# Masked attention stages: VectorE caps the exponentials of every second key block's first pair by a table, in place of TensorE's mask products

## The chip, the cores and the metric

One core of a Trainium2 chip runs the whole program. The metric is device time in microseconds (us) of one execution; the time before is the median of three runs.

## The reference

Four decoder layers run one after the other on x of shape (4, 512, 256): L0 (two attentions with lengths, a small feed-forward), L1 (two masked attentions, then a mixture of experts), L2 (two masked attentions, then a feed-forward), L3 (a causal attention). The change touches the four masked attentions, those of L1 and L2. Cut to what matters:

```python
scores = jnp.einsum('bhqd,bhkd->bhqk', q, k) / jnp.sqrt(jnp.float32(DK))     # 16 heads, DK = 16
scores = jnp.where(mask[:, None, :, :] == 0, NEG, scores)                    # mask of shape (4, 512, 512)
attn = jax.nn.softmax(scores, axis=-1)
out = jnp.einsum('bhqk,bhkd->bhqd', attn, v)
```

## The kernel before

**Stages and units.** The seven attentions are the stages a0 to a6; a2 and a3 (L1) and a4 and a5 (L2) are masked. A stage takes the four batch elements one after the other. Each has four *units* (u = 0 to 3) of four heads, and a unit has eight *halves* (h = 0 to 7): half h belongs to key block kb = h // 2 (128 keys) and to the first or second pair of the unit's heads (h % 2). So the masked stages have 4 x 4 x 4 = 64 units and 512 halves.

**What a half does.** In unit j, TensorE computes for half h the transposed scores, keys on partitions (`key_scores`, L927: two products into one of two double banks of PSUM), then for unit j + 2 the scores with queries on partitions (`query_scores`, L966: two products into a ring of three banks), then for masked stages the mask products of unit j (`key_penalties`, L948: four products of 64 x 64 identity blocks with the transposed mask, added to the transposed scores). VectorE takes the row minimum of each ring bank with the mask added (L1225; scores are held negated), which unit j + 2 will need as its softmax shift, and so frees the bank. ScalarE takes the exponentials of the transposed scores (L1117) into `probT`, which has two slots, one for even and one for odd key blocks. In every even half TensorE multiplies a finished key block of `probT` by V (`outputs`, L987): h = 2, 4 and 6 take the blocks 0, 1 and 2, and the next unit's h = 0 takes block 3. This product waits for the exponentials of both pairs of its block.

**What sets the order.** All engines walk one list made by `schedule` from `timetable`: for each half "ST" (L927), "S" (L966), "exp" (L948 and L1117), then the side work of that half, then "PV" (L987). Side work goes through the same ring of three banks, in the order of the list: in unit 0 the outputs of the batch element before (transposes L1088 and L1092, the output projection L1097, VectorE's reciprocal L1293 and product L1304, and in a4 and a5 a layer norm); in unit 1 the projections q (h = 1) and k (h = 4) of the second half of the heads (L1043); in unit 2 the projection V (h = 1 and 4, L1050) and three of the four mask transposes "mT" (L1056, copied out by ScalarE at L1178); in unit 3 the fourth mT and the transposes of x (L1024) in h = 0, q (h = 4) and k (h = 6). Each unit also turns the minima of another unit (L1232, L1234, then L1011). The last batch element of a block of stages has no next one to prepare, and its units 2 and 3 have no "S" either.

**GpSimd and the DMA queue.** GpSimd turns each mask from integers to bfloat16 (L886, two halves of a batch element) and does parts of the norms. SyncE loads the weights of the coming feed-forward or expert stage into `raw` during a0, a2 and a4 (`load_feed`).

## Time and profile before

| | us |
|---|---|
| median of three runs (2736.17 to 2740.03) | 2736.99 |
| span of the profiled execution | 2740.1 |
| a2 and a3, from their first to their last half, about | 612 (664 to 1276) |
| a4 and a5, about | 606 (1770 to 2376) |
| TensorE busy, whole span | 2505.0 (91%) |
| VectorE busy, whole span | 1783.8 (65%) |
| ScalarE busy, whole span | 1397.9 (51%) |

The page gives the span of the profiled execution, from its first to its last instruction, and no other time for it; it lies 3 us above the median of the runs. "Busy" of TensorE counts a product from its issue to its modelled end, so that consecutive products overlap: the time from one start to the next is what a product costs.

### The profile page before, as it was taken

The page shows a single profiled execution, that of the slowest core. Times are in us where ns is not written, and L with a number is a line of the kernel's source. Part 1 is how long each engine was busy: PE and PEld are TensorE (multiplying, and loading weights), DVE is VectorE, ACT ScalarE, POOL GpSimd, SP SyncE. Part 2 cuts the span into 40 slices and gives each one's busy share as a digit, 9 for nine tenths or more (in the row PEclk, how much of TensorE's full clock was granted, in tenths as well). Part 3 has the DMA queues.
Part 4 walks back from the last instruction along what each step waited for, and adds up shares of the span by engine and source line. Part 5 has one row for each costly group of instructions (what it writes and reads, how often), then busy time and mean ns, then how long its engine had stood idle before and what let it go on. Part 6 is the DMA issues. An engine that isn't in the chain of part 4 may idle for free. (4 is left out here: it accounts for less than half of the span.)

```text
span 2740.1 us, 44289 instructions
## 1 busy us (share of the span) xinstructions
PE 2505.0 (91%) x16014; PEld 1383.7 (50%) x16014; DVE 1783.8 (65%) x4364; ACT 1397.9 (51%) x1921; POOL 739.6 (27%) x867
## 2 busy tenths in 40 slices
PE   6999988989999999997999998799999999797896
PEld 3444433334344444443889998334444444386553
DVE  3566777777777777773557775577777777455554
ACT  1544455545555555565348786155555555452332
POOL 2233334432421111200115664202222111224012
PEclk7999999989999999998899999699999999999999
DMA  6222212112223323220127875423322322001331
GB/s 177 51 50 71 57 45 72 46 45 61 52 82 85 90 68 95 68 64 17 47 70 216 221 220 130 126 60 87 101 67 68 94 68 64 1 9 28 96 84 41
DMA packets 102213, 218.56 MB, mean 80 GB/s; under 512 B 19116, under 2 KB 35372, under 8 KB 100716
## 3 DMA queue, kind: packets, MB, share of 16 engines
q1 hardware_dynamic: 93164, 203.66, 27.0%
q0 software_dynamic: 8832, 12.06, 2.5%
q8 instruction: 129, 2.11, 0.3%
q14 instruction: 88, 0.72, 0.1%
HBM read 100.34 MB, written 12.58 MB: 41 GB/s over the span
## 5 line engine op out<-in xcount | busy, mean ns | idle before, releaser
L1117 ACT ACTIVATE probT_a<-scores 128x1024 f32<-128x1024 f32 (+3 forms) x832 | 786.7, 951 | 733.1 <-PE scores L948 445.2
L1225 DVE CUSTOM_DVE_ANT_0 ring<-ring,maskb_a 128x512 f32<-128x512 f32 x1024 | 680.5, 720 | 176.7 <-PE ring L966 171.1
L966 PE MATMUL ring<-stacks_a 64*128 64x512 f32 (+7 forms) x1664 | 468.3, 411 | 58.8 <-DVE negm_a L1223 26.0
L987 PE MATMUL outputs<-probT_a,V_a 128*32 128x512 f32 (+6 forms) x3328 | 445.6, 579 | 18.5 <-ACT probT_a L1117 9.5
L1223 DVE TENSOR_REDUCE negm_a<-ring 128x1 f32<-128x512 f32 (+3 forms) x640 | 330.8, 564 | 148.9 <-PE ring L972 109.4
L927 PE MATMUL scores<-stacks_a 64*128 64x512 f32 (+7 forms) x1664 | 411.2, 474 | 2.3 <-DMA stacks_a<-narrow_a 2.3
L927 PEld LDWEIGHTS scores<-stacks_a 64*128 64x128 f32 (+1 forms) x1664 | 164.3, 185 | 432.1 <-issue 322.6
L966 PEld LDWEIGHTS ring<-stacks_a 64*128 64x128 f32 (+1 forms) x1664 | 236.2, 191 | 176.6 <-DVE negm_a L1225 72.0
L886 POOL TENSOR_SCALAR maskb_a<-ints_a 128x1024 bf16<-128x1024 int32 x31 | 112.8, 3639 | 409.1 <-DMA ints_a<-in_mask 336.2
L896 POOL TENSOR_TENSOR ve<-mv,epsilon 128x1 f32<-128x1 f32 x96 | 18.2, 190 | 722.5 <-DVE mv L1192 722.5
L948 PE MATMUL scores<-maskT_a,identb 64*64 64x512 bf16 x1024 | 210.2, 401 | 0.0
L948 PE MATMUL scores<-swapped_a,identb 64*64 64x512 bf16 x1024 | 206.7, 401 | 0.0
L1277 DVE SCALAR_TENSOR_TENSOR parts_a<-ring,wcol,parts_a 128x512 fp32r<-128x512 f32 x112 | 83.9, 751 | 186.2 <-ACT parts_a L1166 186.2
L1043 PE MATMUL ring<-xT_a,wt 128*128 128x512 f32 x320 | 169.4, 657 | 25.4 <-DVE xT_a L1265 12.3
L2017 DVE TENSOR_TENSOR hidden_moe<-whole_moe,hidden_moe 128x512 fp32r<-128x512 f32 x124 | 85.9, 692 | 103.2 <-ACT whole_moe L1826 103.2
L1166 ACT ACTIVATE parts_a<-ring,wcol 128x512 fp32r<-128x512 f32 x112 | 77.0, 688 | 148.5 <-PE ring L1043 148.5
L987 PEld LDWEIGHTS outputs<-probT_a,V_a 128*32 128x32 f32 (+1 forms) x3328 | 74.0, 111 | 154.1 <-ACT probT_a L1117 74.0
L1696 PE MATMUL scores<-rowsT_moe,weights_moe 128*128 128x256 f32 x1104 | 147.5, 283 | 0.0
L1225 DVE DVE_READ_ACCUMULATOR2_ANT negm_a<- 128x1 f32 x1024 | 145.6, 142 | 0.0
L1696 PEld LDWEIGHTS scores<-rowsT_moe,weights_moe 128*128 128x128 f32 x1104 | 139.1, 192 | 0.0
L948 PEld LDWEIGHTS scores<-maskT_a,identb 64*64 64x64 bf16 x1024 | 57.8, 103 | 159.1 <-issue 159.1
L1826 ACT ACTIVATE hidden_moe<-scores 128x512 fp32r<-128x512 f32 x124 | 74.1, 598 | 119.4 <-PE scores L1689 59.4
(240 smaller groups left out, 3757.4 us busy)
## 6 DMA issues: line engine op xcount, KB each, us to landing
stacks_a<-parts_a SPq DMA_DIRECT2D x672, 128.0 KB
raw<-in_moew SPq DMA_DIRECT2D x92, 512.0 KB, 4.1
ints_a<-in_mask SPq DMA_DIRECT2D x31, 512.0 KB, 3.5
swapped_a<-maskT_a SPq DMA_DIRECT2D x32, 256.0 KB, 3.7
wt<-in_w SPq DMA_DIRECT2D x7, 1024.0 KB, 4.9
kvT_a<-in_ctxT SPq DMA_DIRECT2D x12, 512.0 KB, 3.3
wrow<-in_row SPq DMA_DIRECT2D x7, 512.0 KB, 6.0
stacks_a<-narrow_a SPq DMA_DIRECT2D x224, 8.0 KB
```

The costliest lines, as they stand in the source:

```text
L886: pool.tensor_scalar(maskb[:, j % 2, 2 * n:2 * n + 2, :], mask_half(j, n)[:, :, :], 0.0, BIG, ALU.is_equal, ALU.mult)\
L927: last = pe.matmul(scores_bank(j, h)[:, e, q0:S], K[rows, g, kb * P:(kb + 1) * P], Q[rows, g, q0:S], start=True, stop=not (a.causal or a.m ...
L948: last = pe.matmul(out[64 * c:64 * c + 64, :], identb[at, at], (maskT if c == e else maskS)[at, m % 2, kb, :], start=False, stop=True)
L966: last = pe.matmul(bank("S", j, n, e)[:, 0:w], Q[rows, g, qt * P:(qt + 1) * P], K[rows, g, 0:w], start=True, stop=not a.causal)
L987: last = pe.matmul(OB[x * slot:(x + 1) * slot, q0:S], V[:, m % 2, kb, c:c + slot], probT[:, kb % 2, x, q0:S], start=(kb == 0), stop=(kb == ...
L1043: last = pe.matmul(out[:, :], wt[:, k, kb, c0:c0 + P], src[:, kb, :], start=(kb == 0), stop=(kb == KB - 1))
L1117: act.activation(probT[:, kb % 2, 2 * p:2 * p + 2, q0:S], scores_bank(j, n)[:, :, q0:S], ACT.Exp, bias=0.0, scale=-1.0).then_inc(c_exp.sem, 1)
L1223: least = dve.tensor_reduce(out, sc, AX.X, ALU.min)
L1225: least = dve.tensor_tensor_reduce(sc, sc, maskb[:, m % 2, qt, :], 1.0, BIG * 2, ALU.add, ALU.min, out)
L1277: dve.scalar_tensor_tensor(out=parts[:, n, low[kind], :], in0=bank(kind, j, n)[:, :], scalar=wcol[:, k, col:col + 1], in1=parts[:, n, high ...
L1696: last = pe.matmul(bank[:, h * SL:(h + 1) * SL], w1(i, a, kb, 2 * q + h), rowsT[:, i % 2, c, kb, :], start=(kb == 0 and (a, c) == PARTS[0] ...
L2017: dve.tensor_tensor(hidden[:, s % 4, 1, :], whole[:, s % 2, :], hidden[:, s % 4, 0, :].bitcast(F32), ALU.subtract).then_inc(m_low, 1)
```

## The change

In the halves h = 2 and h = 6 of every unit of a masked stage (the first pair of key blocks 1 and 3), TensorE's four mask products are left out, and the exponentials are taken of unmasked scores. ScalarE makes a table `caps` beside each copy of the transposed mask, 1 where a key may be seen and exp(-60) where not; VectorE then replaces the pair's exponentials in `probT` by the smaller of them and the table, in place, one instruction of 128 x 1024. VectorE does it one half later (h = 3 and h = 7), behind that half's two row minima, and the product of that key block with V waits for it. The table lies in the upper half of `raw`, so that the lower half alone is loaded early, and the upper half is loaded at the end of the block of stages.

```diff
+RAW_HALF = KB * HID
+MASKED = 60.0
+TAKEN = (2,)
+def taken(a, h):
+    return a.mask is not None and h % 4 in TAKEN
...
-        sp.dma_start(raw[:, 0:hb * P * 2 * KB], io[f"{st}w"]).then_inc(c_raw, 16)
+        size = min(hb * P * 2 * KB, RAW_HALF)
+        sp.dma_start(raw[:, 0:size], io[f"{st}w"][:, 0:size]).then_inc(c_raw, 16)
+    def load_upper(sp, st):
+        src = io["moew"][E:E + 1, :, RAW_HALF:].rearrange("o p n -> (o p) n") if st == "moe" else io[f"{st}w"][:, RAW_HALF:]
+        sp.dma_start(raw[:, RAW_HALF:], src).then_inc(c_rawup, 16)
...
+            caps = raw[:, RAW_HALF:].bitcast(BF16).rearrange("p (m q n) -> p m q n", m=2, q=QT)
...
+            if masked:
+                sp.wait_ge(c_capped.sem, c_capped.count)
+                load_upper(sp, "moe" if first else "f2")
...
+                if not penalised(a, h):
+                    return
...
                 pe.wait_ge(*c_exp.at(j, (kb + 1) * couples - 1))
+                if taken(a, kb * couples):
+                    pe.wait_ge(*c_capped.at(j, kb * couples))
...
-                    act.activation(maskT[:, j % 2, n, :], bank("mT", j, n)[:, :], ACT.Copy).then_inc(c_rA.sem, 1)
+                    act.activation(maskT[:, j % 2, n, :], bank("mT", j, n)[:, :], ACT.Copy)
+                    act.activation(caps[:, j % 2, n, :], bank("mT", j, n)[:, :], ACT.Exp, bias=0.0,
+                                   scale=-MASKED / BIG).then_inc(c_rA.sem, 1)
...
+                if kind == "exp" and n > 0 and capped(j, n - 1):
+                    m, kb = j // 4, (n - 1) // couples
+                    if j % 4 == 0:
+                        dve.wait_ge(*c_rA.at("mT", m, QT - 1))
+                    dve.wait_ge(*c_exp.at(j, n - 1))
+                    given = probT[:, kb % 2, 0:2, :]
+                    dve.scalar_tensor_tensor(out=given, in0=given, scalar=1.0,
+                                             in1=caps[:, m % 2, kb, :].unsqueeze(1).to_broadcast([P, 2, S]),
+                                             op0=ALU.mult, op1=ALU.min).then_inc(c_capped.sem, 1)
...
+                if n == 4:
+                    act.wait_ge(c_rawup, 32)
...
-                    act.wait_ge(c_raw, 32)
+                    act.wait_ge(*((c_raw, 32) if c < 2 else (c_rawup, 16)))
```

TensorE's order in half h = 6 of a unit 1 (L927 the transposed scores, L966 the ring's scores, L948 the mask products, L987 the product with V of block 2), before:

```order
L927 MATMUL scores<-stacks_a 128x512 [waits c_exp]
L927 MATMUL scores<-stacks_a 128x512
L966 MATMUL ring<-stacks_a 128x512 [waits c_rD] x2
L948 MATMUL scores<-maskT_a,identb 64x512
L948 MATMUL scores<-swapped_a,identb 64x512 x2
L948 MATMUL scores<-maskT_a,identb 64x512
L987 MATMUL outputs<-probT_a,V_a 32x512 [waits c_exp]
L987 MATMUL outputs<-probT_a,V_a 32x512 x3
```

and in the changed kernel:

```order
L957 MATMUL scores<-stacks_a 128x512 [waits c_exp]
L957 MATMUL scores<-stacks_a 128x512
L997 MATMUL ring<-stacks_a 128x512 [waits c_rD] x2
L1020 MATMUL outputs<-probT_a,V_a 32x512 [waits c_exp]
L1020 MATMUL outputs<-probT_a,V_a 32x512 x3
```

The four mask products are gone, and the product with V stands right behind the ring's scores. Two halves further on, in h = 0 of the next unit, TensorE's order in the changed kernel is:

```order
L997 MATMUL ring<-stacks_a 128x512 [waits c_rD,c_stack0]
L997 MATMUL ring<-stacks_a 128x512 [waits c_rD]
L980 MATMUL scores<-maskT_a,identb 64x512
L980 MATMUL scores<-swapped_a,identb 64x512 x2
L980 MATMUL scores<-maskT_a,identb 64x512
L1020 MATMUL outputs<-probT_a,V_a 32x512 [waits c_capped,c_exp]
L1020 MATMUL outputs<-probT_a,V_a 32x512 x3
```

Only the wait for `c_capped` is new here; no side work stands between the mask products and the product with V. VectorE's order at the same place in the changed kernel (ISA rows are a row minimum L1260 and the read of its result; L1269 is the cap; L1276 and L1278 turn the minima), from the second minimum of h = 7 to the first of the next unit's h = 1:

```order
L1260 ISA ring,negm_a<-ring,maskb_a 128x512 [waits c_ring]
L1260 ISA negm_a 128x1
L1269 SCALAR_TENSOR_TENSOR probT_a<-probT_a,raw 128x1024 [waits c_exp]
L1260 ISA ring,negm_a<-ring,maskb_a 128x512 [waits c_ring,c_maskb]
L1260 ISA negm_a 128x1
L1260 ISA ring,negm_a<-ring,maskb_a 128x512 [waits c_ring]
L1260 ISA negm_a 128x1
L1276 TENSOR_SCALAR mx_a<-negm_a 128x4x4 [waits c_ring]
L1278 SCALAR_TENSOR_TENSOR mx_a<-negm_a,mx_a 128x4x4
L1260 ISA ring,negm_a<-ring,maskb_a 128x512 [waits c_ring]
```

The cap stands behind the two minima of its half and ahead of those of the next; before, the two groups of minima follow each other directly.

## Rows read from the trace of the kernel before

**Rows 1.** Busy time by stretch: a2-a3, a4-a5; columns named below.

```profile
664.00:1276.00 612.00, 595.77 (x3914) 247.83 (x3913) 423.22 (x1217) 351.70 (x431) 101.16 (x68) 1.00 0.26 70
1770.00:2376.00 606.00, 586.75 (x3825) 243.94 (x3822) 442.85 (x1271) 336.21 (x408) 115.96 (x130) 0.99 0.26 70
```

Its columns are the stretch and its length, then busy us and instruction count of PE, PEld (weight loads), DVE, ACT and POOL, then TensorE's granted clock as a share of 2.4 GHz, the DMA share and GB/s.

**Rows 2.** Timeline of PE, end of a unit 1 in a3: start, us, instruction.

```profile
1029.66 0.74 PE L966 MATMUL ring<-stacks_a 64*128 64x512 f32 x2
1030.34 0.40 PE L948 MATMUL scores<-maskT_a,identb 64*64 64x512 bf16 x1
...
1030.68 1.06 PE L987 MATMUL outputs<-probT_a,V_a 128*32 128x512 f32 x8
```

**Rows 3.** Timeline of DVE at the same place: minima of h = 7, then h = 0.

```profile
1029.71 0.14 DVE L1225 DVE_READ_ACCUMULATOR2_ANT negm_a<- 128x1 f32 x1
1029.71 0.73 DVE L1225 CUSTOM_DVE_ANT_0 ring<-ring,maskb_a 128x512 f32<-128x512 f32 x1
...
1030.36 0.73 DVE L1225 CUSTOM_DVE_ANT_0 ring<-ring,maskb_a 128x512 f32<-128x512 f32 x1
```

**Rows 4.** Waits of PE in a4-a5 (1770 to 2376): us in total, times, longest.

```profile
PE ring L1097 <- DVE o_a L1304: 7.7, 7, 1.1
...
PE ring L1011 <- DVE parts_a L1277: 2.2, 6, 0.6
PE outputs L987 <- ACT probT_a L1117: 2.1, 6, 0.4
```

**Rows 5.** Waits of PE in a2-a3 (664 to 1276).

```profile
PE ring L1011 <- DVE parts_a L1277: 3.9, 7, 0.6
```

**Rows 6.** Single source lines: count, duration ns min/median/max, first and last start.

```profile
L1204 DVE TENSOR_TENSOR X<-X,probT_a x4: 1225/1225/1226, 1716.1 to 1732.2; 128x1024 f32<-128x1024 f32 x4
L1844 DVE TENSOR_TENSOR weights_moe<-raw,weights_moe x96: 1209/1225/2253, 1297.3 to 1687.7; 128x1024 fp32r<-128x1024 f32 x96
L1178 ACT ACTIVATE maskT_a<-ring x64: 570/591/598, 637.3 to 2300.9; 128x512 bf16<-128x512 f32 x64
L886 POOL TENSOR_SCALAR maskb_a<-ints_a x31: 3627/3637/3674, 609.5 to 2275.0; 128x1024 bf16<-128x1024 int32 x31
```

**Rows 7.** Timeline of PE, a unit 2 in a3: h = 3 to the product of block 1.

```profile
1037.84 0.40 PE L966 MATMUL ring<-stacks_a 64*128 64x512 f32 x2
...
1039.86 1.99 PE L1050 MATMUL ring<-wt,kvT_a 128*128 128x256 f32 x8
...
1042.01 1.07 PE L987 MATMUL outputs<-probT_a,V_a 128*32 128x512 f32 x8
```

**Rows 8.** Timeline of PE, h = 0 of the unit 3 that follows it.

```profile
1049.03 0.40 PE L1056 MATMUL ring<-identb,maskb_a 128*128 128x128 bf16 x4
1049.55 0.66 PE L1024 MATMUL ring<-identf,xs_a 128*128 128x128 f32 x4
```

**Rows 9.** Timeline of DVE, a unit 0 in a5: h = 3 and h = 4.

```profile
2322.16 0.42 DVE L1304 TENSOR_TENSOR o_a<-ring,rinv_a 128x256 f32<-128x256 f32 x1
...
2323.96 0.42 DVE L1315 TENSOR_TENSOR junk<-ring,wrow 128x256 f32<-128x256 f32 x1
```

**Rows 10.** Timeline of PE, the same unit 0: first output projection, in h = 4.

```profile
2322.79 1.13 PE L1097 MATMUL ring<-wt,oTn_a 128*128 128x256 f32 x4
```

**Rows 11.** Page, DMA issues: count, KB each, median us to landing.

```profile
raw<-in_moew SPq DMA_DIRECT2D x92, 512.0 KB, 4.1
```

**Rows 12.** Timeline of POOL and DVE at the start of the expert stage.

```profile
1296.14 1.89 POOL L1612 TENSOR_TENSOR area_moe<-X,rs 128x1024 f32<-128x1024 f32 x1
...
1297.31 1.81 DVE L1844 TENSOR_TENSOR weights_moe<-raw,weights_moe 128x1024 fp32r<-128x1024 f32 x1
```

**Rows 13.** Busy time by stretch of 1 us, near the end of a5 (columns of rows 1).

```profile
2342.00:2343.00 1.00, 1.00 (x8) 0.00 (x0) 0.09 (x2) 0.57 (x2) 0.00 (x0) 0.50 0.00 0
```

**Rows 14.** Timeline of PE around it, with the wait ahead of the first.

```profile
2340.20 0.49 PE L966 MATMUL ring<-stacks_a 64*128 64x512 f32 x1 [0.69 <-DVE negm_a L1225]
...
2341.62 1.93 PE L987 MATMUL outputs<-probT_a,V_a 128*32 128x512 f32 x8
```

More of the change, by code:

```diff
@@ L319, in build @@
     c_maskb = tally("c_maskb")
+    c_capped = tally("c_capped")
     c_early = sem("c_early")
@@ L343, in build @@
     c_rawb = sem("c_rawb")
+    c_rawup = sem("c_rawup")
     c_turned = Signal(sem("c_turned"), {}, 1, token_blocks)
@@ L458, in load_feed @@
         if st == "moe":
-            sp.dma_start(raw[:, :], io["moew"][E:E + 1, :, :].rearrange("o p n -> (o p) n")).then_inc(c_raw, 16)
+            sp.dma_start(raw[:, 0:RAW_HALF], io["moew"][E:E + 1, :, 0:RAW_HALF].rearrange("o p n -> (o p) n"))\
+                .then_inc(c_raw, 16)
             return
@@ L555, in stack_transfers, with capped @@
             return 9 if att[units[j // 4][0]].length or fresh(j) else 7
+        def capped(j, h):
+            return taken(att[units[j // 4][0]], h)
         for kind, j, n in work:
@@ L560, in attention_block @@
                 c_exp.mark(j, n)
+                if capped(j, n):
+                    c_capped.mark(j, n)
             if kind == "PV":
@@ L914, in bank_free, with penalised @@
                     pe.wait_ge(*given.at(*before))
+            def penalised(a, h):
+                return a.causal or a.mask is not None and not taken(a, h)
             def key_scores(j, h):
@@ L927, in key_scores @@
                     last = pe.matmul(scores_bank(j, h)[:, e, q0:S], K[rows, g, kb * P:(kb + 1) * P],
-                                     Q[rows, g, q0:S], start=True, stop=not (a.causal or a.mask is not None))
-                if not (a.causal or a.mask is not None):
+                                     Q[rows, g, q0:S], start=True, stop=not penalised(a, h))
+                if not penalised(a, h):
                     last.then_inc(c_st.sem, 1)
@@ L937, in key_penalties @@
                 q0 = a.since(kb)
+                if not penalised(a, h):
+                    return
                 if a.mask is not None and u == 0 and h == 0:
@@ L949, in key_penalties @@
                                              (maskT if c == e else maskS)[at, m % 2, kb, :], start=False, stop=True)
-                if a.causal or a.mask is not None:
-                    last.then_inc(c_st.sem, 1)
+                last.then_inc(c_st.sem, 1)
             def query_scores(j, n):
```

## The prediction

> **What bounds the kernel now.** I read four views: busy time by stretch, to see which engine is full where the change acts; TensorE's timeline, to see what a mask product costs there; VectorE's timeline at the same place, to see what the cap would be put in front of; and the waits of TensorE, to see where it already stands still.
>
> In the masked stages TensorE is full: 595.77 of 612 us and 586.75 of 606 us busy, at a granted clock of 1.00 and 0.99 [rows 1]. VectorE has 423.22 and 442.85 us of work there (69 and 73%), ScalarE 351.70 and 336.21 (57 and 55%). So a product removed from TensorE is worth its time, and VectorE has room on average: 128 caps at the price taken below are 157 us, 866 + 157 = 1023 of 1218 us. The average does not decide, however. TensorE's ring banks are freed by VectorE's minima, and the row of the second score product (0.74 us, against 0.40 for a pair that does not wait) shows that TensorE already waits for the bank that the first minimum frees [rows 2, 3, 7]: that minimum's result is read from 1029.71 to 1029.85, and 0.15 us later, at about 1030.00, the second product starts. VectorE is then back to back until the next half: the minima start at 1029.71 and 1030.36, one every 0.65 us [rows 3]. The cap is put at the end of just such a run.
>
> **What is removed.** The four mask products of a half run side by side: they start at 1030.34, and the next product starts at 1030.68 [rows 2], so a half's mask costs 0.334 us, not four times 0.40. 128 halves of 512 lose it: 128 x 0.334 = 42.7 us. Not all lies on the path. In h = 2 of the 16 units 1 the transposes of the minima (L1011) already wait for VectorE, seen 6 and 7 times [rows 4, 5]: there TensorE would only wait longer (16 halves). In units 2 and 3 of the last batch element of a3 and a5 the product with V waits for the exponentials (L987 on L1117) [rows 4] (8 halves). In h = 2 of 14 units 3 the product of block 0 waits for an earlier copy (L1126) in some; I count half of them (7). That leaves 97 x 0.334 = **32.4 us** gained.
>
> **What a cap costs.** There is no such instruction in the trace. The nearest row has the same 128 x 1024 elements, also in place and with two inputs: 1.225 us, four times within 1 ns; a second line of that size has a median of 1.225 [rows 6]. A lower bound is one half of it, if two elements went per cycle (0.61); an upper one the longest of those 96, 2.25. I take 1.225, the exact shape, and since consecutive VectorE instructions overlap by 0.73 - 0.65 = 0.08 us [rows 3], the queue behind it moves by 1.145.
>
> **What the caps add, place by place.** The cap stands behind two minima and ahead of the next two, so everything behind it on VectorE is late by 1.145 us unless VectorE was idle; TensorE feels it where a ring bank or the product with V is due at once.
>
> - *h = 6 of 16 units 1 and 14 units 3.* In the following unit's h = 0 the product of block 3 comes right behind the mask products, at 1030.68 [rows 2]. The cap can start when h = 7's second minimum is through, at 1030.36 (where h = 0's first minimum starts now [rows 3]), ends at 1031.585, and with the hand-over of 0.15 the product starts at 1031.73: 1.05 us late. 30 x 1.05 = 31.5 us.
> - *h = 6 of 14 units 2.* In the next h = 0 the last mask transpose and the transposes of x come first. The first of x starts at 1049.55, although the mask transposes before it began at 1049.03 and cost some 0.33 [rows 8]: it already waits 0.19 us for the bank of h = 0's first minimum. That minimum is behind the cap, so the whole 1.15 is added: 14 x 1.15 = 16.1 us. The product of block 3 then finds its cap done.
> - *h = 2 of 15 units 0.* The projection L1097 of h = 4 at 2322.79 [rows 10] needs the product L1304, which ends at 2322.16 + 0.42 = 2322.58 [rows 9]. 0.21 us between them, less 0.15 for the hand-over and with some room in the ring, leave 0.2 to 0.3 us of slack, so the cap ahead of L1304 costs 0.86 in the 8 units without a layer norm (6.9 us). In the 7 units of a4 and a5 with one, VectorE is the bound in unit 0: the L1097 waits of 7.7 us, 7 times [rows 4], are all there, and the layer norm's first product follows the minima at 2323.96 [rows 9]. There the first cap costs 0.92 and the second, in h = 6, its full 1.15: 7 x 2.07 = 14.5 us.
> - *Four more without cover* (two in the first unit 0 of a4, which has no side work; one in h = 2 of unit 1 of each last batch element): 4 x 1.05 = 4.2 us.
> - *58 caps at no cost*, and their cover: in h = 4 of 14 units 2 the projection V takes 1.99 us between the scores and the product of block 1; from h = 3's scores at 1037.84 to that product at 1042.01 there are 4.17 us, time for two minima, the cap and 1 us more [rows 7]. The same cover is k in 14 units 1 and q in 14 units 3. Eight caps in h = 6 of units 0 lie beside the output projections, eight in the drained tails above. Without that cover each would cost 1.05, some 60 us in all.
>
> Sum of the added stalls: 31.5 + 16.1 + 6.9 + 14.5 + 4.2 = **73.2 us** at 70 places.
>
> **What else is added or moved.** 64 exponentials of 128 x 512 for the table, at the 0.591 us of the copies beside them [rows 6]: 38 us on ScalarE, which is idle over 40% of the time. Each holds its ring bank 0.59 us longer; the next user comes over 1 us later, so I count nothing (if it were all paid, 38 us; this is not in the range). Loading the lower half of `raw` early moves fewer bytes. The upper half, 1 MB in one transfer of SyncE's queue, goes behind the last cap at about 1276; half of that size lands in 4.1 us [rows 11], two of them would be 8, and the weights of the expert stage are first split at 1297.3 [rows 6]: hidden, with some 13 us to spare. VectorE's wait for the table in a unit 0 is long met. At the ends of the blocks nothing is queued behind SyncE's new wait but the next block's loads.
>
> **The sum.** 73.2 - 32.4 = +40.8 us. The profiled execution's span of 2740.1 would become 2781; the median of the runs lies 3 us below it, and from 2736.99 I get **2778 us**, 1.5% slower. This case's own range is 2758 to 2811: the low end if all 42.7 us of mask products are gained and the second cap of the layer-norm units costs 0.4 instead of 1.15 (another 5) with some slack at the 14 units 2; the high end if the clock falls ten times (below, 14 us) and GpSimd holds up some caps (18 us).
>
> **The rivals.** A measurement of this kernel tells about 0.2% (5.5 us) from no change.
>
> *The cap is cheap: faster.* The stalls are 70 times the cap's price less 12.5 us (70 x 1.225 - 12.5 = 73.2). At half the price, 0.61 us, they are 30 us, and 2737 - 32 + 30 = 2735; with all 42.7 us gained, 2724. The change wins from a price under (32.4 + 12.5) / 70 = 0.64 us. Against it: two lines of this very size and 1.21 to 1.23 us in both [rows 6]; the cap's table is bfloat16, though, and read twice over, which no row has. The same outcome comes if the order has more slack than I see at the 30 places. 0.10 for faster, 0.09 for no change.
>
> *GpSimd holds the caps up: slower still.* An instruction of VectorE that began at 1297.31, while GpSimd was in one of two inputs (1296.14 to 1298.03), took 1.81 us in place of 1.225: it ended 1.09 us behind GpSimd's end [rows 12]. A mask conversion lasts 3.64 us [rows 6], 32 in all, and one that met a cap could hold it up by as much; if 4 to 8 of them do, +14 to +28 us: 2792 to 2806. Against it: by the order the conversions stand some 5 us away from the caps of the units 0, and most caps have cover. 0.13.
> The Trainium skill ("SBUF — State Buffer", section "Who interferes with whom") says that a VectorE instruction with two inputs in SBUF contends with a GpSimd instruction that reads SBUF, and that the second to issue is blocked for the whole of the first. By that rule the minima of now, with one input in PSUM, are free of it and the caps are not, which speaks against this change; the row at 1297.31 agrees with it.
>
> *TensorE's clock falls at the new stalls.* After a wait of 0.69 us at 2340.20 the product with V at 2341.62 took 1.93 us instead of 1.06 to 1.07 [rows 2, 7, 14], in a stretch at a granted clock of 0.50, the 1.2 GHz level [rows 13]. Such a fall costs about 1.4 us there. In the masked stages the clock is 1.00 now in spite of the short waits, and a new stall of 1.05 us leaves TensorE busy for 20 us around it. With 10 to 30 falls, 14 to 41 us: 2792 to 2819. 0.10.
>
> *The removed products don't come free, or the upper load is late:* 2790 to 2795 for the latter, 0.02.
>
> **How the numbers follow.** Likeliest case 0.56, the slower rivals 0.25, in all 0.81 slower; 0.09 the same, 0.10 faster. The predicted time is the likeliest case's, 2778. The range goes down to 2736, to take in the no-change side, and up to 2812; outside lie the faster case and the far end of the clock.
>
> **What would show it.** Right: the four mask products' lines with 1536 products in place of 2048; a cap of about 1.22 us; waits of TensorE at the product with V on the cap's line, some 34 of about 1.05 us; waits of about 1.2 us at the transposes of x in units 3, and longer ones at the projection L1097 in units 0; VectorE some 157 us busier, TensorE's clock near 1.00. Wrong: a cap of some 0.6 us; caps with no waits behind them at these places; a clock well under 1.00 in the masked stages, or caps of 2 us and more beside mask conversions.

## The result, and the profile after

The changed kernel takes 2825.25 us (median of four runs, 2822.25 to 2831.87), the kernel before on the same chip 2738.51 us: a ratio of 1.0313, interval 1.0292 to 1.0334. It is 86.7 us slower. The forecast was 41 us slower, with a range that ended at 2812: the direction was right, the size was half of what came, and the range did not hold it.

The profiled execution of the changed kernel has a span of 2820.4 us, 80.3 more than the one of before. First the stretches that answer to [rows 1], from 10 us ahead of a2's first half to the end of a3, and the same for a4 and a5 (columns as there):

```profile
658.00:1307.00 649.00, 588.18 (x3658) 243.76 (x3658) 490.86 (x1281) 362.24 (x459) 102.02 (x68) 0.99 0.25 64
1803.00:2453.00 650.00, 579.21 (x3569) 240.11 (x3569) 511.00 (x1337) 348.21 (x436) 116.09 (x130) 0.98 0.24 64
```

612 us have become 649 and 606 have become 650: the loss is in the masked stages. TensorE's busy time fell by only 7.6 us in each, and its share from 97 to 91 and 89%: it now waits. VectorE has 68 us more in each, still only 76 and 79% of the stretch. Then the cap's own line (count, ns min/median/max, first and last start), and who waited for it:

```profile
L1269 DVE SCALAR_TENSOR_TENSOR probT_a<-probT_a,raw x128: 1218/1220/1582, 677.7 to 2452.6; 128x1024 f32<-128x1024 f32 x128
...
  PE outputs L1020: 41.2, 51
```

The price of a cap was taken right (1.22 us against 1.225 in [rows 6]), and the product with V waits for it 51 times, 41 us in all (some 34 times had been forecast). The longest waits of TensorE in a2-a3 and in a4-a5 (us in total, times, longest), to be held against [rows 4] and [rows 5]:

```profile
PE outputs L1020 <- DVE probT_a L1269: 20.2, 25, 1.6
...
PE ring L1057 <- DVE negm_a L1260: 6.4, 6, 1.2
PE ring L1044 <- DVE parts_a L1321: 6.3, 7, 0.9
PE ring L1130 <- DVE o_a L1348: 6.0, 14, 0.7
```

```profile
PE outputs L1020 <- DVE probT_a L1269: 21.0, 26, 1.6
PE ring L1130 <- DVE o_a L1348: 14.7, 14, 1.4
PE ring L997 <- DVE negm_a L1260: 7.8, 8, 1.1
PE ring L1057 <- DVE negm_a L1260: 7.4, 6, 1.2
PE ring L1044 <- DVE parts_a L1321: 4.7, 7, 0.9
```

L1057 (the transposes of x), L1130 (the output projection) and L1269 are the three waits that the prediction named. The transposes of the minima, L1044, wait longer than before (6.3 against 3.9 us, 4.7 against 2.2): there the time of the removed products has simply become a wait.

Now the place that the prediction worked out most closely, h = 7 of a unit 1 and h = 0 of the unit 2 behind it (timeline of TensorE and VectorE; it answers to [rows 2] and [rows 3]):

```profile
1045.23 0.73 DVE L1260 CUSTOM_DVE_ANT_0 ring<-ring,maskb_a 128x512 f32<-128x512 f32 x1
...
1045.88 1.22 DVE L1269 SCALAR_TENSOR_TENSOR probT_a<-probT_a,raw 128x1024 f32<-128x1024 f32 x1
...
1047.02 0.69 DVE L1260 CUSTOM_DVE_ANT_0 ring<-ring,maskb_a 128x512 f32<-128x512 f32 x1
1047.24 1.06 PE L1020 MATMUL outputs<-probT_a,V_a 128*32 128x512 f32 x8 [0.99 <-DVE probT_a L1269]
```

The cap runs from 1045.88 to 1047.10, the product starts 0.14 us behind it, after a wait of 0.99, and the next minimum starts 1.14 us behind the cap's start, all as forecast.

**A table of halves.** Each half begins with its transposed scores (L927, L957 after), so the time from one such start to the next is what a half costs. In the half above, for instance, the starts are 1044.85 and 1048.24, 3.39 us; before, the same half took 2.34. Summed over the 16 batch elements of the masked stages, after less before, us:

| place | forecast | after | e1 | e2 | e3 | e9 |
|---|---|---|---|---|---|---|
| h = 2 and h = 6 of all units (products removed) | -32.4 | -8.3 | -8.8 | 0.7 | 1.1 | -8.2 |
| h = 0 of units 0 and 2 (the product waits for the cap) | 31.5 | 30.8 | 0.0 | 30.8 | 2.7 | 8.2 |
| h = 0 and 1 of units 3 (transposes of x) | 16.1 | 23.3 | 1.1 | 23.4 | 27.4 | 1.8 |
| h = 4 of units 0 (output projection) | 14.4 | 14.9 | 0.0 | 14.9 | 17.1 | 3.7 |
| h = 0 and 1 of units 1 | 9.1 | 14.1 | 1.4 | 15.5 | 16.9 | 5.8 |
| h = 4 of units 1 to 3 | 2.1 | 5.0 | -0.1 | 5.4 | 3.1 | 3.1 |
| all other halves | 0 | 0.9 | 1.4 | -0.3 | 12.6 | 9.3 |
| sum | 40.8 | 80.7 | -5.0 | 90.4 | 80.9 | 23.7 |

(e1 to e9 are the experiments below; differences against the one profiled execution of before. That execution spent 5.7 us more than the changed kernel's ahead of a2, and the changed kernel's 5.4 us more behind a3 and a5; these nearly cancel, so the masked stages' 80.7 us are the span's 80.3. The medians differ by 6 us more because of the executions that were profiled: the changed kernel's is its fastest, 3 us under its median, and that of before lies some 3 us above its own. The profiled execution of e1 is the slowest of its seven: a2's first batch element is 2.7 us longer in it, with four halves at a granted clock of 0.50 to 0.80, and the other 15 are 7.6 us shorter.)

The column of after tells where the forecast failed: the added stalls came to 89 us where 73 were expected, and **the removed products brought 8 us where 32 were expected**. That was the question for the experiments.

### The profile page after: what moved, and what is told of

Read it like the earlier page. It is cut to its first block and busy times, and to the rows that moved or that the text cites. A ratio compares the mean times of both kernels' runs of the same rounds, so it can differ in the third digit from the quotient of the medians.

```text
span 2820.4 us, 43620 instructions
## 1 busy us (share of the span) xinstructions
PE 2488.8 (88%) x15502; PEld 1376.6 (49%) x15502; DVE 1919.4 (68%) x4492; ACT 1423.7 (50%) x1985; POOL 740.6 (26%) x867
## 5 line engine op out<-in xcount | busy, mean ns | idle before, releaser
L1260 DVE CUSTOM_DVE_ANT_0 ring<-ring,maskb_a 128x512 f32<-128x512 f32 x1024 | 684.1, 717 | 170.2 <-PE ring L997 166.2
L957 PE MATMUL scores<-stacks_a 64*128 64x512 f32 (+7 forms) x1664 | 414.5, 477 | 2.5 <-DMA stacks_a<-narrow_a 2.5
L957 PEld LDWEIGHTS scores<-stacks_a 64*128 64x128 f32 (+1 forms) x1664 | 165.7, 187 | 437.8 <-issue 304.9
L1269 DVE SCALAR_TENSOR_TENSOR probT_a<-probT_a,raw 128x1024 f32<-128x1024 f32 x128 | 156.7, 1224 | 37.5 <-ACT probT_a L1150 37.5
L980 PE MATMUL scores<-maskT_a,identb 64*64 64x512 bf16 x768 | 158.6, 403 | 0.0
L980 PE MATMUL scores<-swapped_a,identb 64*64 64x512 bf16 x768 | 156.1, 403 | 0.0
L1260 DVE DVE_READ_ACCUMULATOR2_ANT negm_a<- 128x1 f32 x1024 | 145.3, 142 | 0.0
L1890 DVE TENSOR_TENSOR weights_moe<-raw,weights_moe 128x1024 fp32r<-128x1024 f32 x96 | 119.2, 1242 | 23.0 <-ACT weights_moe L1840 23.0
```

The costliest lines, as they stand in the source:

```text
L957: last = pe.matmul(scores_bank(j, h)[:, e, q0:S], K[rows, g, kb * P:(kb + 1) * P], Q[rows, g, q0:S], start=True, stop=not penalised(a, h))
L980: last = pe.matmul(out[64 * c:64 * c + 64, :], identb[at, at], (maskT if c == e else maskS)[at, m % 2, kb, :], start=False, stop=True)
L1260: least = dve.tensor_tensor_reduce(sc, sc, maskb[:, m % 2, qt, :], 1.0, BIG * 2, ALU.add, ALU.min, out)
L1269: dve.scalar_tensor_tensor(out=given, in0=given, scalar=1.0, in1=caps[:, m % 2, kb, :].unsqueeze(1).to_broadcast([P, 2, S]), op0=ALU.mult, ...
L1890: dve.tensor_tensor(weights[:, (i + 1) % 2, 1, quarter(c)], raw[:, quarter(c)], weights[:, (i + 1) % 2, 0, quarter(c)].bitcast(F32), ALU.s ...
```

## The experiments

*Theory A:* the mask products stood in time in which TensorE would have waited anyway, so taking them away is worth some 8 us, and everything else is the caps. *Theory B*, the prediction's: the removal is worth 32 us, and then the caps cost some 119. *Theory C:* the loss is not at the caps, but in the table's exponentials on ScalarE, the loads of `raw`, or the clock.

**e1, the removal alone.** The kernel before with

```diff
+            def penalised(a, h):
+                return a.causal or a.mask is not None and h % 4 != 2
```

in place of the condition for a mask product.

> The kernel before, with the four mask products of h = 2 and h = 6 left out in every masked unit and nothing in their place (those pairs of heads are not masked): no caps, no table, no change to the loads. Theory A (the products stood in time in which TensorE would wait anyway, for a ring bank or for the exponentials of the half before): about 9 us faster than before, 2725 to 2733, and new waits of 0.1 to 0.3 us behind the ring's scores in those halves. Theory B (the prediction: 97 of 128 halves gain 0.334 us): 32 us faster, about 2706. All 128 gained: 2696.

Measured 2729.56 us, ratio 0.9962 (0.9949 to 0.9976): 7 to 14 us faster, 8 by the medians. Theory A, and far from the 32 us of B. The two waits that eat the rest can be read off. In h = 6 of a unit 1 nothing stands between the mask products and the product with V. The kernel before, timeline of ScalarE and TensorE:

```profile
1026.11 1.02 ACT L1117 ACTIVATE probT_a<-scores 128x1024 f32<-128x1024 f32 x1 [1.33 <-PE scores L948]
...
1026.99 0.40 PE L948 MATMUL scores<-maskT_a,identb 64*64 64x512 bf16 x1
...
1027.33 1.07 PE L987 MATMUL outputs<-probT_a,V_a 128*32 128x512 f32 x8
```

and e1 at the same place (the ScalarE row holds two exponentials, of h = 5 and 6, 0.97 us apart):

```profile
1025.14 1.94 ACT L1122 ACTIVATE probT_a<-scores 128x1024 f32<-128x1024 f32 x2 [1.32 <-PE scores L954]
1025.36 0.73 PE L971 MATMUL ring<-stacks_a 64*128 64x512 f32 x2
1026.22 1.06 PE L992 MATMUL outputs<-probT_a,V_a 128*32 128x512 f32 x8
```

In e1 the exponential of the half before ends at about 1025.14 + 1.02 = 1026.16, and the product starts 0.06 us later: it cannot come earlier, whatever is taken out in front of it. Before, that exponential ended at 1027.13 and the product started at 1027.33. So only 0.20 less 0.06, that is 0.14 us, were to be had, not 0.334; the half became 0.15 us shorter. The other wait is the ring's. h = 2 of a unit 2, before:

```profile
958.13 0.50 PE L927 MATMUL scores<-stacks_a 64*128 64x512 f32 x2
...
959.71 0.40 PE L1056 MATMUL ring<-identb,maskb_a 128*128 128x128 bf16 x4
```

and in the changed kernel:

```profile
970.79 0.50 PE L957 MATMUL scores<-stacks_a 64*128 64x512 f32 x2
...
972.38 0.40 PE L1089 MATMUL ring<-identb,maskb_a 128*128 128x128 bf16 x4 [0.21 <-DVE negm_a L1260]
```

The mask transpose comes 1.58 us behind the half's start before, 1.59 after: it needs the bank that this half's first minimum frees, and that minimum has not moved. The half gained nothing, though TensorE had four products less. In e1 the halves h = 2 of the units 2 have the same wait of 0.21 and gain 0.00.

**e2, the caps alone.** The changed kernel with the mask products kept:

```diff
-                return a.causal or a.mask is not None and not taken(a, h)
+                return a.causal or a.mask is not None
```

> The changed kernel with the mask products kept in all halves: table, caps and their waits are added and nothing is taken away (the caps change nothing in the result). Theory A: the changed kernel's time plus the 9 us, about 2834 (2828 to 2842), caps alone costing some 95 us. Theory B: the removal is worth 32 us, so 2857. Theory C (most of the loss is not at the caps but in ScalarE's 64 table exponentials, the upper load or the clock) says the same as A here and differs in the next run.

Measured 2830.83 us, ratio 1.0334 (1.0314 to 1.0354): 93 us more than before, and 6 more than the changed kernel. Removal and caps add up: -8 + 93 = 85 of the 86.7 us. The table's column e2 is that of after, place by place, with the first line at nothing. Theory B is out.

**e3, the queue without the wait.**

```diff
-                if taken(a, kb * couples):
+                if taken(a, kb * couples) and (j + 3) // 4 not in units:
...
-                    dve.scalar_tensor_tensor(out=given, in0=given, scalar=1.0,
+                    dve.scalar_tensor_tensor(out=caps[:, m % 2, 0:QT:2, :], in0=given, scalar=1.0,
```

> The changed kernel, where each cap reads the pair and the table as before but writes to a part of the table that nothing reads, and the product with V does not wait for it (save in the units 1 to 3 of a block's last batch element), so that blocks 1 and 3 are not masked for the first pair: VectorE's queue is as loaded as in the changed kernel, only the wait of the product is gone. Theory A: the places where the product itself waits (h = 0 of units 0 and 2, 31 us in the table of halves) go, those where VectorE's queue holds up a ring bank or the output projection stay: about 2794 (2785 to 2805). Rival A2 (the delay of the minima alone costs it all, the product would have waited for them anyway): 2825. Theory C: near 2825 as well.

Measured 2814.54 us, ratio 1.0269 (1.0248 to 1.0290): 11 us less than the changed kernel, where 31 were expected. The caps last as long as before (median 1.222 us), and the waits of the product with V did go (30.8 to 2.7 us in the table). But the time came back further on. In e3, behind h = 7 of a unit 1:

```profile
960.64 1.22 DVE L1269 SCALAR_TENSOR_TENSOR raw<-probT_a,raw 128x1024 bf16<-128x1024 f32 x1
960.95 1.07 PE L1020 MATMUL outputs<-probT_a,V_a 128*32 128x512 f32 x8
...
961.78 0.69 DVE L1260 CUSTOM_DVE_ANT_0 ring<-ring,maskb_a 128x512 f32<-128x512 f32 x1
...
962.29 0.80 PE L997 MATMUL ring<-stacks_a 64*128 64x512 f32 x2
```

The product now runs beside the cap, but the minimum at 961.78 frees the bank late, and h = 1's pair of scores takes 0.80 us instead of 0.40. Of 1.05 us, 0.39 come back there in units 0 and 2, and 0.5 more in h = 2 of eight units 0. So the wait for the cap hid a second delay of the same origin, and each alone costs part of the sum. The clock took more: e3's stretches are

```profile
658.00:1303.00 645.00, 598.12 (x3656) 247.93 (x3654) 488.40 (x1277) 360.79 (x457) 102.08 (x68) 0.98 0.25 65
1796.00:2452.00 656.00, 599.64 (x3581) 246.12 (x3581) 509.69 (x1337) 349.85 (x437) 116.14 (x130) 0.96 0.24 64
```

with a mean granted clock of 0.96 in a4-a5, against 0.98 in the changed kernel and 0.99 before: TensorE's clock fell in h = 0 of nine units 3, where it was six in the changed kernel, and in h = 1 of five units 1 of a4 and a5, which are 2.5 to 2.8 us longer than before (0.7 to 0.9 in the changed kernel). Rival A2 and theory C gave 2825; 2814.5 lies nearer to them than to A's 2794, so this run alone does not decide. With the places it does: the queue costs more than theory A had given it.

**e4, the cap one half earlier in VectorE's order.** Behind its own half's minima, ahead of the next half's:

```diff
-                if kind == "exp" and n > 0 and capped(j, n - 1):
+                if kind == "exp" and capped(j, n):
...
-                    dve.wait_ge(*c_exp.at(j, n - 1))
+                    dve.wait_ge(*c_exp.at(j, n))
```

> The changed kernel with the cap put one half earlier in VectorE's order, behind its own half's minima and ahead of the next half's. Theory A: VectorE is idle there for part of the time (0.5 to 0.9 us before the first minimum of h = 7), so a cap holds up the next minima by about 0.55 instead of 1.15 us and the product with V finds it done: some 40 to 50 us of stalls less 9, 2765 to 2785. A rival that each cap costs its full time wherever it stands: 2825.

Measured 2781.83 us, ratio 1.0142 (1.0114 to 1.0171): half the loss, at the upper edge of what was expected. So the place in the queue decides, and a cap does not cost its time wherever it stands. The halves showed where most of the remainder was: 27 us in h = 0 and 1 of the units 2, almost all in a2 and a3. There (timeline of GpSimd, VectorE and TensorE):

```profile
959.02 1.89 POOL L892 TENSOR_TENSOR xs_a<-X 128x1024 f32<-128x1024 f32 x1
...
959.09 2.90 DVE L1269 SCALAR_TENSOR_TENSOR probT_a<-probT_a,raw 128x1024 f32<-128x1024 f32 x1
...
962.72 0.79 PE L997 MATMUL ring<-stacks_a 64*128 64x512 f32 x1 [2.02 <-DVE negm_a L1260]
```

The cap began 0.07 us behind GpSimd's squares of x and took 2.90 us: it ended 1.08 us behind GpSimd's end at 960.91, as the row of before at 1297.31 had ended 1.09 behind one ([rows 12]). The Trainium skill ("SBUF — State Buffer", section "Who interferes with whom") has this rule: an instruction of VectorE with two inputs in SBUF and one of GpSimd that reads SBUF exclude each other, and the second waits for the whole of the first. For GpSimd's squares the trace agrees with it, in five caps of 2.8 to 2.9 us. For its mask conversions, which read SBUF too, it does not. In the changed kernel:

```profile
850.77 3.65 POOL L912 TENSOR_SCALAR maskb_a<-ints_a 128x1024 bf16<-128x1024 int32 x1 [28.39 <-DMA ints_a<-in_mask]
...
851.97 1.22 DVE L1269 SCALAR_TENSOR_TENSOR probT_a<-probT_a,raw 128x1024 f32<-128x1024 f32 x1
```

This cap ran wholly inside a conversion and took its usual time, as two more did (at 933.70 and 1176.08). Only caps that began soon after a conversion's start were held up: 0.33 and 0.71 us behind it they took 1.79 and 1.41 (e3), 0.83 behind it 1.28 (changed kernel), all ending 2.1 us behind that start. Here the measurement decides: a conversion of 3.64 us held a cap up by 0.6 us at most.

**e9, the collision taken away.** As e4, and GpSimd's squares wait for that cap:

```diff
+                        if j - 2 in units and att[units[j - 2][0]].mask is not None:
+                            pool.wait_ge(*c_capped.at(4 * (j - 2) + 1, 6))
                         pool.tensor_tensor(xs[:, :, :], tiles, tiles, ALU.mult).then_inc(c_squares.sem, 1)
```

> The variant with the cap one half earlier (e4), where GpSimd's squares of x for the norm of the batch element after next wait for the cap of h = 6 of unit 1. In e4 five caps in a2 and a3 lasted 2.8 to 2.9 us instead of 1.22 beside that instruction, and the halves h = 0 and 1 of units 2 were 23 us longer. If the collision is the cause: about 2760 (2754 to 2766). If not: 2782 as e4.

Measured 2763.48 us, ratio 1.0074 (1.0058 to 1.0089). The collision was the cause: the longest cap is now 1.61 us, and the 27 us are 7. With an earlier place and no collision with the squares the caps cost some 30 us instead of 89 (21.7 us more than before by the medians, and the 8 that the removal gives), but still more than the removal brings.

**e5, the products twice.** The kernel before, with the four products of h = 2 and h = 6 issued twice:

```diff
-                        for c in range(2):
+                        for c in range(4 if h % 4 == 2 else 2):
+                            more, c = h % 4 == 2 and c < 2, c % 2
...
-                                             (maskT if c == e else maskS)[at, m % 2, kb, :], start=False, stop=True)
+                                             (maskT if c == e else maskS)[at, m % 2, kb, :], start=False, stop=not more)
```

> The kernel before, with the four mask products of h = 2 and h = 6 issued twice (the mask is added twice, the result is the same). Theory A (in these halves TensorE is at the edge of a wait of 0.2 to 0.33 us, which the products fill): taking them away gained 8 us, but another set has no wait left to fill and costs nearly all of 128 x 0.334 = 43 us, less some 4 where VectorE's parts are waited for: 2772 to 2782. If mask products in these halves were not on TensorE's path at all: 2738. If removal and addition were worth the same: 2746.

Measured 2757.27 us, ratio 1.0056 (1.0043 to 1.0070): 15.5 us more on a median of before of 2741.75, where 34 to 44 were expected. The halves give the reason: h = 6 became 0.22 us longer in 51 of the 64 units (14.0 us in all; nothing in units 0 of a4 and a5), h = 2 by 0.22 in 14 units 3 (3.1 us) and by 0.09 or less in nearly all others. So a second set costs 0.22 us where it costs anything, not 0.334, and in h = 2 of units 0 to 2 two sets still fit into the wait, or nearly. Theory A's statement on the sizes was wrong here; that three quarters of the h = 2 products can be taken away or doubled for 0.09 us or less supports its cause.

**e6, only the places with cover.**

```diff
+COVERED = ((1, 2), (2, 2), (3, 2))
...
-    return a.mask is not None and h % 4 in TAKEN
+    return a.mask is not None and h % 4 in TAKEN and (u, h) in COVERED
```

> The changed kernel with the caps and the removed products in h = 2 of units 1 to 3 alone (48 of 128), where projections of 2 us stand ahead of the product with V. Theory A: 42 of the caps cost nothing, 6 in last batch elements 1.05 us each (6 us), and the removed products bring only 0.11 in units 3 (2 us): 2742 (2738 to 2747). Theory B: the same 6 us, less 0.334 for some 25 of them (8 us): 2736. A rival in which every cap costs 0.7 us wherever it stands: 2772.

Measured 2749.86 us, ratio 1.0030 (1.0020 to 1.0040), 8 us slower on a median of before of 2741.75; expected were some 4 us more. The halves show parts of the expected size, but not all where they were expected: 5.3 us in h = 4 at five places (1.00 to 1.09 each), -1.8 in h = 2, and 0.6 elsewhere. The five are the units 1 of the last batch element of each block, the units 3 of the last but one, and the first unit 2 of a2. In the units 3 of the last batch element but one the profile of before shows no projection q in h = 4, and so no cover. So the other 43 caps of 1.22 us did cost nothing, and removing the products there brought 0.1 us in one place of three. The other 4 us lie outside the masked stages in the profiled execution, and their cause is open.

**e7, e10, e11, e13: the caps on GpSimd.** VectorE is left as before, GpSimd multiplies by the table:

```diff
+                if kind == "exp" and capped(j, n):
+                    m, kb = j // 4, n // couples
+                    if j % 4 == 0:
+                        pool.wait_ge(*c_rA.at("mT", m, QT - 1))
+                    pool.wait_ge(*c_exp.at(j, n))
+                    given = probT[:, kb % 2, 0:2, :]
+                    pool.tensor_tensor(given, given, caps[:, m % 2, kb, :].unsqueeze(1).to_broadcast([P, 2, S]),
+                                       ALU.mult).then_inc(c_capped.sem, 1)
```

> The changed kernel with the caps on GpSimd (exponentials times table, which has the same effect) in its order right behind the exponential, so that VectorE has only its work of before. Theory A: the stalls come from VectorE's queue alone, so they go and the 8 us of the removed products stay, unless a cap on GpSimd lasts longer than the 2.2 us from the end of the exponential to the product of block 3 (GpSimd's 128 x 1024 products of two inputs last 1.89 us): 2730, and up to 2755 if it is some 0.5 us late at the 44 places of h = 6. Theory C (ScalarE's table, loads, clock): as the changed kernel, 2825.

Measured 2817.12 us, ratio 1.0272 (1.0258 to 1.0286), a miss: near theory C's number, for another reason. The product with V hardly waits for a cap any more (L1028 on L884, 1.6 us in each block of stages). But 63 us are in h = 1 of 14 units 2, which took 7.4 us on average instead of 2.9. GpSimd's order there (a3), and what VectorE waited for in a4-a5:

```profile
969.73 2.14 POOL L884 TENSOR_TENSOR probT_a<-probT_a,raw 128x1024 f32<-128x1024 f32 x1 [7.64 <-ACT probT_a L1158]
971.95 3.64 POOL L920 TENSOR_SCALAR maskb_a<-ints_a 128x1024 bf16<-128x1024 int32 x1
```

```profile
DVE ring L1268 <- POOL maskb_a L920: 25.5, 7, 3.7
```

The second mask conversion, which the next batch element's minima need, had come behind a cap that itself waits for an exponential. e10 puts the cap one half later in GpSimd's order, so that the conversion is first:

```diff
-                if kind == "exp" and capped(j, n):
-                    m, kb = j // 4, n // couples
+                if kind == "exp" and n > 0 and capped(j, n - 1):
+                    m, kb = j // 4, (n - 1) // couples
```

> The caps on GpSimd as in e7, but one half later in its order, so that the second mask conversion (side work of h = 6 in units 1) comes ahead of the cap and no longer behind it. In e7 the halves h = 1 and 2 of the 14 units 2 became some 68 us longer, with VectorE waiting for that conversion. If the order of the conversion is the cause, and the caps themselves (2.13 us) are in time for the product with V: e7 less 68, about 2750 (2742 to 2757); the halves of h = 6 keep the small gains of the removed products, and in units 0 of a4 and a5 the layer norm waits behind caps on GpSimd (10 us in e7). If GpSimd's caps are late in themselves: above 2780.

Measured 2762.19 us, ratio 1.0081 (1.0066 to 1.0095): the 63 us are gone, so the order was the cause. It is 5 us above the expected interval; 15 us are in h = 1 of units 1 in a4 and a5, behind the layer norm of units 0. e11 leaves the mask products in units 0 of a4 and a5:

```diff
-    return a.mask is not None and h % 4 in TAKEN
+    return a.mask is not None and h % 4 in TAKEN and not (u == 0 and a.ln)
```

> As e10, but in units 0 of a4 and a5 the mask products stay and there are no caps, so that the layer norm does not wait on GpSimd. Theory A: only the removed products' gains are left, less small waits at the last batch elements: 4 to 8 us faster than before, 2734 to 2738. That removed products pay 0.334 us once no cap is in VectorE's way: some 30 us faster, 2710.

Measured 2741.69 us, ratio 1.0002 (0.9993 to 1.0011): no difference, where 4 to 8 us were expected. The table, its exponentials and its loads are all in this run, which takes the time of before: of theory C the clock's part is left, and at most some 3 us of the loads (below). e13 leaves them also in the first unit 0 of a2, where a1's layer norm still runs:

```diff
+        def after_norm(m, u):
+            return None if u == 0 and units[m] == ("a2", 0) else u
...
+    return a.mask is not None and h % 4 in TAKEN and not (u == 0 and a.ln or u is None)
```

> As e11 (caps on GpSimd, none in units 0 of a4 and a5), and without caps also in unit 0 of the first batch element of a2, where the layer norm of a1 still runs: in e11 that batch element was 6 us longer than before, while the other 15 were each about 0.5 us shorter. If that is all: 4 to 8 us faster than before (ratio 0.997 to 0.9985), the version that keeps the removed products' 8 us and pays nothing. If the sum of small delays on GpSimd eats it: no difference again (0.9995 to 1.0005).

Measured 2736.79 us, ratio 1.0003 (0.9988 to 1.0018): again none, so no version was found that beats the kernel before. In the halves 13 of the 16 batch elements are 0.4 to 0.6 us shorter than before, some 7 us, but a2's first one is 5 us longer and the parts behind a3 and a5 are 3 us longer. With 112 caps or fewer off VectorE there is nothing left to lose, and also nothing won.

**e12, all mask products left out.**

```diff
-                return a.causal or a.mask is not None and h % 4 != 2
+                return a.causal
```

> The kernel before with all mask products left out (no pair is masked), nothing in their place. It bounds what any such replacement could win. All 512 x 0.334 on the path: 171 us faster, 2570. Theory A: in odd halves the ring bank for the next half's second product, freed by VectorE, sets the time and nothing is gained; in even halves the exponential before the product with V now comes earlier too, so that up to 0.334 is gained in part of the 256: 30 to 85 us faster, 2655 to 2710. If even that is held up elsewhere: 2720 or more.

Measured 2697.09 us, ratio 0.9836 (0.9820 to 0.9852): 44 us faster, where 512 sets at 0.334 us would be 171. In the halves the odd ones are 89.0 us shorter and the even ones 47.7 longer. Most odd halves without products let the next one start 0.43 us earlier, and that one then waits some 0.3 for its bank, as theory A had it. In this order of the work it bounds what any replacement of these products can win, however cheap: 44 us for 512 sets, 0.09 us each.

## Why the prediction was right and wrong

**The removed products: the step that failed.** "128 halves of 512 lose it ... That leaves 97 x 0.334 = 32.4 us gained." Alone they are worth 8 us (e1): 0.08 to 0.15 us in h = 6 of 52 of the 64 units (0.35 in two of them) and 0.11 in h = 2 of units 3, and next to nothing in the other h = 2. The prediction had looked for a wait of TensorE in the profile of before, found it in 31 of the 128 halves, and took the rest for free of one. It did not ask what each product behind the removed ones would have to wait for once it could come 0.334 us earlier. The rows to answer that were there: the exponential of the half before ended 0.20 us ahead of the product with V, and the mask transposes already waited some 0.13 us for their bank (they start 0.58 us behind the product ahead of them, and 0.45 in e5). A wait that is absent from the view because work fills it is found only by computing the next releaser's time.

**The cap's price: right.** 1.225 us taken, 1.22 measured; the rival of a cheap cap fell with it.

**The stalls: right in place, 16 us short in sum.** 30.8 us against 31.5 at the products of block 3. The 14.9 against 14.4 at the output projection in h = 4 of units 0 are in part luck: 14 places took 0.88 to 0.95 as forecast, but the first unit 0 of a2 took 2.44 instead of 0.86 (granted clock 0.76) and that of a4 nothing instead of 1.05. Three terms were too small. In h = 0 of units 3 the stall is 1.10 us as forecast (1.15), but in six of the 14 it is 2.1 to 2.4, because TensorE's clock fell behind it (below): 23.3 us instead of 16.1. In the eight units 0 without a layer norm of their own the second cap was called covered by the output projections. In seven of them the unit 1 behind became 0.33 us longer (2.3 us), and behind the first of a2 it became 2.7 us longer, where a cap met a product of GpSimd (below) and the clock fell to 0.65: 5 us missed. And three caps of h = 2 that the prediction had called covered cost 1.05 to 1.09 us each: those of the units 3 of the last batch element but one, where no projection q stands in h = 4, and the first of a2's units 2: 3 us.

**What was called covered: right in the main.** Of the 48 caps of h = 2 in units 1 to 3, 43 cost nothing (e6). The table's exponentials cost nothing that the halves show: e6 has all 64, and outside the places named its halves are 0.6 us longer in sum. For the upper load the runs tell less: behind a3 and a5 the profiled executions of the ten runs with it are 0.8 to 7.6 us longer than before, those of the three without it (e1, e5, e12) -1.1 to 3.4, so that some 3 us stay open.

**The rivals.** GpSimd's contention hardly happened in the changed kernel: 126 caps took 1.22 us, one 1.28, and one 1.58. The last began inside a product of GpSimd and ended 1.09 us behind that product's end, as the row at 1297.31 had in the prediction:

```profile
690.90 0.72 POOL L929 TENSOR_TENSOR X<-xh,wrow 128x256 f32<-128x256 f32 x1
...
691.13 1.58 DVE L1269 SCALAR_TENSOR_TENSOR probT_a<-probT_a,raw 128x1024 f32<-128x1024 f32 x1
```

The conversions that the rival counted on, at up to 3.64 us each, did not do this (see e4). With the squares it was missed by a hair: they end at 963.60 + 1.89 = 965.49 and the cap starts at 965.50.

```profile
963.60 1.89 POOL L892 TENSOR_TENSOR xs_a<-X 128x1024 f32<-128x1024 f32 x1
...
965.50 1.22 DVE L1269 SCALAR_TENSOR_TENSOR probT_a<-probT_a,raw 128x1024 f32<-128x1024 f32 x1
```

In e4, with the cap earlier, it came at once. The clock's fall did happen, in part. A unit 3 of a4, h = 0, changed kernel:

```profile
2117.60 1.22 DVE L1269 SCALAR_TENSOR_TENSOR probT_a<-probT_a,raw 128x1024 f32<-128x1024 f32 x1
...
2119.54 1.48 PE L1057 MATMUL ring<-identf,X 128*128 128x128 f32 x8 [1.24 <-DVE negm_a L1260]
...
2120.94 1.94 PE L1020 MATMUL outputs<-probT_a,V_a 128*32 128x512 f32 x8
```

```profile
2120.00:2123.00 3.00, 3.00 (x16) 0.83 (x16) 1.18 (x5) 0.62 (x2) 0.00 (x0) 0.59 0.65 169
2120.94:2122.88 1.94, 1.94 (x11) 0.28 (x10) 0.69 (x1) 0.00 (x0) 0.00 (x0) 0.50 0.68 173
```

After the wait of 1.24 us the product with V takes 1.94 us, at a granted clock of 0.50, the 1.2 GHz level, over its own time and a mean of 0.59 over these 3 us. Most such halves are 1.3 us longer than one without the fall (2.42 against 1.10 over before), close to the 1.4 us of the prediction's rival; the six make up the 7 us that the term for units 3 lacked. Seven of the other eight units 3 kept the full clock, and in e2 it fell in six again, three of them others; no run shows what decides.

## What to carry to other kernels

Work that is taken off a full engine is worth only what lies between its end and the next thing that the engine would wait for: before counting n times its price, compute for the instruction behind it when its other inputs and its buffer are ready, since a busy share of 97% says nothing of that. The same work put on an engine with 30% idle time costs its price at the point where it stands if that engine's results free the first one's buffers; its place in the order is worth as much as its length (89 us of stalls became about 30 by one place earlier, once GpSimd's squares kept out of its way). And such a move is best bounded first by leaving the work out altogether: e1 and e12 show in one run each what it can win in this order.

## What the runs showed of the hardware that was not expected

A second set of the same four 64 x 64 products right behind the first cost 0.22 us, the first 0.334 from its start to the next product's start (e5). An instruction of VectorE with two inputs in SBUF, 1.22 us alone, took 2.8 to 2.9 us when it began just after one of GpSimd of 1.89 us (e4), while the row minima, with one input in PSUM, ran beside the same instruction at their usual 0.70 us (changed kernel, at 964.24). It took 1.22 us inside a mask conversion of GpSimd that had begun 1.2 us earlier, and up to 1.79 where the conversion had begun less than 0.9 us earlier (changed kernel, e3). GpSimd's product of 128 x 1024 by a bfloat16 table took 2.13 us, against 1.89 for its float32 squares of the same size (e7).
